# Another slot plan for the work that runs beside the shared FFN in a decoder layer on one core

## The reference

```python
x = x + attn(layernorm(x))            # 32 query heads, 8 key heads, causal, rotary
x = x + xattn(layernorm(x), ctx_2048) # both sides rounded to fp8 and back, then multiplied
x = x + moe(layernorm(x))             # 8 experts, top 1, capacity 256, and a shared FFN
```

```python
q = (xb * (448 / amax)).astype(float8_e4m3fn); xq = q * (amax / 448)   # per 128 numbers
x = x + einsum('emk,enk->emn', xq, wq)                                   # wq from ctx_2048
probs = softmax(xt @ Wg); eidx = argmax(probs)                           # xt = layernorm(x)
pos = cumsum(one_hot(eidx)) ...; keep = pos < 256                        # runs over all tokens
shared = silu(xt @ sw1) * (xt @ sw3) @ sw2                               # 704 hidden columns
```

## Time and profile before

| | us |
|---|---|
| median of 3 runs | 1579.77 (1578.70 to 1581.19) |
| the profiled execution | 1581.1, its span 1579.3 |
| PE busy | 1453.4 (92%) |
| DVE busy | 1205.1 (76%) |
| POOL busy | 1022.9 (65%) |
| ACT busy | 959.4 (61%) |
| granted TensorE clock, mean | 0.97 |

### The profile page before, as it was taken

The page is one execution under the profiler, slowest core; times in us unless marked ns, Lnnn a source line. Parts: engine busy times, 40 slices in busy tenths (PEclk is TensorE's granted clock), DMA queues, the critical chain, the costliest instruction groups (busy, mean ns, idle before and its releaser), DMA issues.

```text
span 1579.3 us, 26942 instructions
## 1 busy us (share of the span) xinstructions
PE 1453.4 (92%) x8617; PEld 1274.5 (81%) x8617; DVE 1205.1 (76%) x2936; ACT 959.4 (61%) x2420; POOL 1022.9 (65%) x1006
## 2 busy tenths in 40 slices
PE   5899999999999999999999997758988887999997
PEld 4788888888878888888888886648888787899996
DVE  7678888887887887887887887976676755577775
ACT  4687777777676787887887886432121213556562
POOL 3787887887777888888898896732121213345555
PEclk9999999999999999999999999888999999899998
DMA  6435534333322433433443432121000003577766
GB/s 205 139 101 165 158 103 128 116 85 109 115 60 59 107 105 90 115 98 95 115 111 86 113 94 67 54 83 60 27 28 28 8 28 124 179 228 223 228 214 237
DMA packets 106812, 177.08 MB, mean 112 GB/s; under 512 B 16886, under 2 KB 38646, under 8 KB 106672
## 3 DMA queue, kind: packets, MB, share of 16 engines
q1 hardware_dynamic: 103920, 166.84, 35.8%
q0 software_dynamic: 2560, 8.25, 1.6%
q10 hardware_dynamic: 192, 0.26, 0.1%
HBM read 97.31 MB, written 31.98 MB: 82 GB/s over the span
## 4 chain that ended last, share of the span: by engine, by line
PE 67%; DVE 15%; ACT 8%; issue 4%; DMA 3%; POOL 2%; SPq 1%; DVEq 0%; ACTq 0%; POOLq 0%
PE bank L429 15%; PE bank L431 14%; PE bank L430 14%; PE bank L481 6%; PE bank L447 4%; PE bank L496 4%; PE bank L497 4%; PE bank L448 4%; ACT P L811 3%; DVE P L1110 2%; PE bank L421 1%; ACT xnx L833 1%; DVE Opair L1145 1%; ACT Otmp L817 1%; DVE work L1059 1%
## 5 line engine op out<-in xcount | busy, mean ns | idle before, releaser
L811 ACT ACTIVATE P<-P,mn 128x512 f32<-128x512 f32 (+3 forms) x512 | 284.8, 557 | 210.5 <-DVE mn L1110 206.6
L1532 POOL TENSOR_TENSOR P<-P,ri 128x128 f32<-128x128 f32 (+3 forms) x512 | 361.4, 737 | 22.4 <-DVE ri L1099 22.3
L1110 DVE CUSTOM_DVE_ANT_0 P<-bank,mask 128x512 f32<-128x512 f32 (+3 forms) x512 | 236.6, 480 | 97.2 <-PE bank L448 95.6
L1151 DVE TENSOR_TENSOR PTl<-bank,PTh 128x512 fp32r<-128x512 f32 (+1 forms) x384 | 229.8, 599 | 33.5 <-ACT PTh L823 30.9
L481 PE MATMUL bank<-ident,P 128*128 128x128 f32 x1280 | 202.6, 273 | 2.5 <-POOL P L1532 2.5
L823 ACT ACTIVATE PTh<-bank 128x512 fp32r<-128x512 f32 (+1 forms) x384 | 197.9, 516 | 6.3 <-PE bank L481 3.2
L447 PE MATMUL bank<-KT,QT 128*128 128x256 f32 (+2 forms) x512 | 188.7, 369 | 10.9 <-DVE mn L1110 10.9
L496 PE MATMUL bank<-PTh,VS 128*128 128x256 f32 (+2 forms) x512 | 163.2, 329 | 13.0 <-DVE PTl L1151 8.9
L429 PE MATMUL bank<-XT,Wh 128*128 128x512 f32 x384 | 162.8, 424 | 9.3 <-DVE XT L1081 3.5
L448 PE MATMUL bank<-KT,QT 128*128 128x256 f32 (+2 forms) x512 | 166.3, 325 | 0.0
L497 PE MATMUL bank<-PTl,VS 128*128 128x256 f32 (+2 forms) x512 | 156.9, 327 | 0.0
(11 more groups left out here) (202 smaller groups left out, 4231.9 us busy)
## 6 DMA issues: line engine op xcount, KB each, us to landing
RW<-in_wf SPq DMA_DIRECT2D x170, 256.0 KB, 3.1
QT<-qh SPq DMA_DIRECT2D x256, 64.0 KB, 2.0
QT<-ql SPq DMA_DIRECT2D x252, 64.0 KB, 2.0
Oraw<-in_wo SPq DMA_DIRECT2D x16, 512.0 KB, 5.3
KT<-KT SPq DMA_DIRECT2D x32, 256.0 KB, 3.0
xnx<-in_ctx SPq DMA_DIRECT2D x32, 256.0 KB, 3.5
Wraw<-in_wqkv SPq DMA_DIRECT2D x9, 768.0 KB, 5.0
saved<-Wh SPq DMA_DIRECT2D x7, 768.0 KB, 3.5
```

The costliest lines, as they stand in the source:

```text
L811: e.activation(pq, pq, ACT.Exp, bias=mn[:, z, qb:qb + 1], scale=-1.0, accum_out=rs[:, z, qb:qb + 1]).then_inc(a_exp, 1)
L1110: e.tensor_tensor_reduce(P[:, z, off[qb]:off[qb] + k], bank[n % 2][:, 0:k], mask[:, 512 - k:512], -0.125, BIG, ALU.add, ALU.min, mn[:, z, ...
L1151: e.tensor_tensor(pt_part(PTl, part), bank[2 + part][:, 0:128 * n].rearrange("p (m n) -> p m n", n=128), pt_part(PTh, part).bitcast(F32), ...
L1532: e.tensor_tensor(pq, pq, ri[:, z, qb:qb + 1].to_broadcast([128, n]), ALU.mult).then_inc(g_norm, 1)
```

## The change

Only numbers in `slots()` change. The instructions are the same ones, and their operands too. For batch 0 nothing moves but its `place`, by one slot. For batches 1 to 3, with s the base slot:

| stage | before | after |
|---|---|---|
| context_turn i | s - 4, - 3, - 2, 0 | s - 9 + i |
| cross_round i | s - 1 + i | s - 7 + 2i |
| cross_turn i | s + 1 + i | s - 5 + 2i |
| cross_product i | s + 2 + i | s - 4 + 2i |
| stats2 i, norm2 | s - 13 + i, s - 7 | s - 12 + i, s - 8 |
| rstd3, norm3, route_turn | s + 6, + 7, + 9 | s + 4, + 5, + 7 |
| logits, choose | s + 12, + 14 | s + 10, + 12 |
| place | s + 19 (b = 3: s + 15) | s + 17 (b = 3: s + 14) |

So for batch 2 (s = 16) the roundings stand in slots 9, 11, 13 and 15, the cross turns in 11, 13, 15 and 17, the products in 12, 14, 16 and 18. The core of the diff:

```diff
-            plan(s - 13 + i if b else s - 3 + i // 2, "stats2", b, i)
-            plan(s + 1 + i, "cross_turn", b, i)
-            plan(s + 2 + i, "cross_product", b, i)
-            plan(s - 1 + i, "cross_round", b, i)
...
+            if b:
+                plan(s - 12 + i, "stats2", b, i)
+                plan(s - 9 + i, "context_turn", b, i)
+                plan(s - 7 + 2 * i, "cross_round", b, i)
+                plan(s - 5 + 2 * i, "cross_turn", b, i)
+                plan(s - 4 + 2 * i, "cross_product", b, i)
...
+        plan(s - (8 if b else 2), "norm2", b)
+        plan(s + (4 if b else 6), "rstd3", b)
+        plan(s + (14 if b == NB - 1 else 17 if b else 18), "place", b)
```

More of the change, by code:

```diff
@@ L43, in slots @@
         for i in range(TB):
-            plan(s - 13 + i if b else s - 3 + i // 2, "stats2", b, i)
-            plan(s + 1 + i, "cross_turn", b, i)
-            plan(s + 2 + i, "cross_product", b, i)
-            plan(s - 1 + i, "cross_round", b, i)
[L48 to L57, removed]
+            if b:
[4 more added lines that the diff above has]
+                plan(s - 4 + 2 * i, "cross_product", b, i)
+            else:
+                plan(s - 3 + i // 2, "stats2", b, i)
+                plan(s - 4 + i + i // 3, "context_turn", b, i)
+                plan(s - 1 + i, "cross_round", b, i)
+                plan(s + 1 + i, "cross_turn", b, i)
+                plan(s + 2 + i, "cross_product", b, i)
+            plan(s + (5 if b else 7) + i // 2, "norm3", b, i)
+            plan(s + (7 if b else 9) + i // 2, "route_turn", b, i)
+        plan(s - (8 if b else 2), "norm2", b)
+        plan(s + (4 if b else 6), "rstd3", b)
+        plan(s + (10 if b else 12), "logits", b)
+        plan(s + (12 if b else 14), "choose", b)
+        plan(s + (14 if b == NB - 1 else 17 if b else 18), "place", b)
     for i in range(2):
```

## The result

| | before | after |
|---|---|---|
| median of 20 runs each | 1580.6 (1578.7 to 1584.6) | 1586.1 (1580.1 to 1591.2) |
| ratio, 95% interval | | 1.0029 (1.0018 to 1.0039) |
| the profiled execution, its span | 1581.1, 1579.3 | 1580.8, 1579.0 |
| granted clock, mean of that execution | 0.97 | 0.971 |
| PE, DVE busy | 1453.4, 1205.1 | 1453.1, 1201.9 |

The forecast was 1574. The last two rows of the table say little; the one of the profiled execution says something new: in the changed kernel it is one of the fastest. Its 20 runs spread over 11 us, and they follow the mean granted clock: the spans average 1578.7 us at 0.973 (2 runs), 1580.8 at 0.971 (4), 1582.3 at 0.970 (2), 1583.9 at 0.969 (2), 1585.1 at 0.968 (8) and 1588.8 at 0.966 (2). Span times mean clock is an estimate of the time at the full clock.

What follows compares the result with a forecast made beforehand. PE, 92% busy, bounds the kernel, so its idle or slow stretches in the FFN count. Removing 39.6 us and adding 33.4 nets -6.2 us: 1573.6 against the median, taken as 1574, range 1561 to 1587.

Steps and rivals of the forecast that it cites:

- What the change removes: PE's waits between 1067 and 1306 us go, -25.1 us, with the low clock behind them, -10.2; moved context turns -1.4.
- all four kinds: PE waits: first cross turn 11.6 us, `place` 3.8, product behind `place` 7.6, first FFN step of a batch 2.1.
- The read-out behind a rounding: In the FFN, eight products wait 2.0 us each for DVE's late read-out, 16 us; 17.5 with batch 1's other waits.
- The third turns: Slots 7, 8, 23, 24: third turn waits 1.75 or 2.95 us for the first's read-out; with clock falls +12.8 us.
- The clock: Behind the eight product waits in the FFN the sum let the granted clock stand, adding nothing.
- Rival One: The eight product waits lower the clock, 1.7 us each: 1587 if all, about 1580 if three or four; chance 0.30.
- Ahead of the FFN: Before x = 0, a rounding and four more read-outs start the FFN 3.1 us later; bounds -1 to +6.
- The prediction's other sum, 1576.5: The whole sum if POOL's port sharing stretched the rounding ahead of the FFN by 2.9 us.
- Where the experts begin: At the experts' first turn, `place` wait of 1.42 us goes and tokens' wait shrinks by 1.5: gain 2.9 us.
- rival Four: The start ahead of the FFN grows by 6 us and the end gives only 1: 1578.5; chance 0.15 with rival three.

Runs made afterwards that it cites:

- the early context turns: Changed kernel with the first three context turns of batches 2 and 3 three slots earlier: 1570.69 us, ratio 0.9934.
- the last kernel: Changed kernel with context turns early, batches 1 and 2 begun later, turns and products one slot later, batch 3's routing and row loads early: 1556.06 us, ratio 0.9848.

## Why the prediction was wrong

**What the change removes** was right in kind, and in size for the waits: all four kinds went, but for 0.44 us. The low clock that went with them was one fall more than the sum had, since in batch 1 it lasted 6.8 us (length, then PE, PEld, DVE, ACT and POOL busy, clock, in the kernel before):

```profile
1091.90:1098.70 6.80, 5.28 (x15) 4.34 (x16) 6.56 (x12) 1.01 (x2) 4.74 (x5) 0.50 0.00 1
```

**The read-out behind a rounding** was right in place and nearly in size: eight waits, 15.7 us in all (16.4 in the two rows less 0.61 at x = 0, and rounding), forecast 8 x 1.85 = 14.8 as the profile shows idle time. What is above is one wait of 2.99 where 1.9 were expected. There POOL's rounding lies beside DVE's subtraction for the FFN, which takes 1.11 us; the same instruction took 0.39 us six microseconds before, with POOL idle:

```profile
1085.59 0.39 DVE L1352 TENSOR_TENSOR Hl<-hm,Hh 128x256 fp32r<-128x256 f32 x1
1091.63 1.11 DVE L1352 TENSOR_TENSOR Hl<-hm,Hh 128x256 fp32r<-128x256 f32 x1
```

```profile
1091.20 1.26 POOL L1580 TENSOR_TENSOR work<-work 128x512 f32<-128x512 f32 x1 [10.68 <-DVE work L1185]
```

The subtraction ends at 1092.74, 0.28 us behind POOL's instruction (1092.46). Of the 1.1 us in question 0.72 is this stretch, and the rest is the subtraction itself, which doesn't stand in the slot of the 1.81 us wait. The Trainium skill, page "SBUF — State Buffer", section "Who interferes with whom", says that a DVE instruction with two SBUF inputs contends with a GpSimd instruction that reads SBUF. The trace agrees, by 0.72 us here. The prediction had named the effect for the start and as a bound here, and had put it into neither number.

**The third turns** were right: 1.50 and 2.75 twice each, forecast 1.75 and 2.95, and a fall behind one of the two longer ones in the profile.

**The clock** is the step that failed most: the sum let it stand after the eight product waits, a term of nothing. The prediction asked of each wait whether it is long enough to bring the clock down, found 2.00 us with no fall and 2.17 us with one, put its eight waits of 1.85 on the safe side, and left the falls to a rival with 0.30. But no safe side shows at such a length. In one execution 1.81 and 1.78 us brought it down and 1.83 and 1.78 did not. The very wait that the prediction took for its safe side, the 2.00 us at 462.12 in the attention, which the change doesn't touch, is followed by the lower clock in the changed kernel's profile (12 matmuls where the kernel before gets 21 through):

```profile
461.37 0.47 PE L434 MATMUL bank<-XT,Wh 128*128 128x512 f32 x1 [2.02 <-DVE XT L1086]
462.30:465.60 3.30, 3.30 (x12) 2.83 (x11) 1.17 (x5) 1.41 (x4) 3.30 (x4) 0.50 0.50 165
```

Over many executions about half of the eight bring it down, by the price of 1.7 us a fall: filling them with work gave 7.8 us back. Two rows on either side of a supposed edge were read as the edge. The right value for such waits was an expected share of falls, four of eight, times 1.7 us: 6.8 us, and the forecast would have been 1580.8. Rival One had this price, near 1580 for three or four.

**Ahead of the FFN** the sum said +3.1, and it was +5.9. PE's rows there, and DVE's between them:

```profile
1064.05 1.09 PE L426 MATMUL bank<-ident,XN 128*128 128x128 f32 x4 [6.25 <-issue]
1070.09 1.09 PE L426 MATMUL bank<-ident,XN 128*128 128x128 f32 x4 [2.40 <-issue]
1072.64 0.55 PE L434 MATMUL bank<-XT,Uh 128*128 128x256 f32 x1 [0.61 <-issue]
```

```profile
1058.81 1.48 DVE L1064 TENSOR_SCALAR work<-X,mv,rstd 128x512 f32<-128x512 f32 x1
1062.92 0.43 DVE L1185 TENSOR_SCALAR work<-work 128x512 f32<-128x512 f32 x1
1066.41 2.97 DVE L1343 TENSOR_TENSOR Dl<-RW,Dh 128x512 fp32r<-128x512 f32 x2
```

```profile
1058.30 1.71 POOL L1617 TENSOR_TENSOR Dl<-RW,Dh 128x512 fp32r<-128x512 f32 x1
1067.12 3.40 POOL L1617 TENSOR_TENSOR Dl<-RW,Dh 128x512 fp32r<-128x512 f32 x2
```

The chain of seven turns was as drawn. Late are two of DVE's steps, both beside POOL's splitting: the rounding, forecast to end at 1061.5, ends at 1063.3 (it begins 0.8 us late, and its first instruction takes 1.48 us; it took 0.54 in the earlier trace rows), and the two pieces take 2.97 where two lone ones of 0.68 would take 1.4. These 1.8 and 1.6 us cover the 2.8 between 1069.8 and 1072.64. The prediction's other sum, 1576.5, stretched the rounding by 2.9 us; its instructions grew by 0.9, and the pieces by 1.6. That batch 1's work is what stands in the way is shown: with it moved behind x = 0, the start is 1063.70, and the same first instruction takes 0.54.

**Where the experts begin** I forecast -1.5 for the tokens' wait, and it was +0.5. SP issued the load at 1331.37, 1.4 us earlier than in the earlier trace rows; the tokens let the turn start 0.8 us earlier, and PE got there 1.3 us earlier, so nothing closed. That the schedule sets this wait, and nothing that the load itself needs, is shown: with the stages one to three slots and the load two slots earlier it is gone.

**In the FFN of the profiled execution** the misses nearly cancel, to +0.7 us. Three falls behind product waits, which the sum had at nothing, are +5.1; one fall instead of two behind third turns is -1.7, and the one fall more of before up to -1.7. The idle time in all went from 26.5 to 25.4 us where 26.9 were forecast, -1.5.

So rival One and rival Four both came true in part. From 1573.6 to 1586.1 it is 12.5 us: 2.8 at the start, 0.7 in the FFN, 2.0 and 0.5 at the end, and 5.3 of clock in the median that the profiled execution doesn't have. The last 1.3 are what the sum took off because the profiled execution of before lay above the median of 3 runs; against the median of 20 it lies 0.5 above.

Still open: how often each single wait brings the clock down, for which one profile of each kernel is too few; and which falls the early context turns save.

## What to carry to other kernels

When stages share an in-order engine, list for each slot what that engine does ahead of the one instruction that the busiest engine waits for; moving one culprit away helps only if nothing else of the same length takes its slot. Where several short waits per stage are near the length that has once been seen to drop TensorE's clock, price each with a chance of a fall, and check the spread of the run times against the mean granted clock before trusting one profile; span times mean clock, averaged over the runs, tells the waits of two kernels apart from their clock. And a filler of useless matmuls is a cheap experiment that separates the clock's share of a wait from the wait itself.

## What the runs showed of the hardware

- Idle times of TensorE of equal length (1.78 and 1.78 us, 1.81 and 1.83 us, in slots of the same kind) are followed by the lower clock once and by the full one the other time. The changed kernel's 20 runs range from a mean clock of 0.973 to 0.966 and by 11 us with it; the last kernel, with fewer long waits, stays at 0.976 to 0.979 and within 3 us in its 5 runs.
- The same wait in the attention, 2.00 us before and 2.02 after, was followed by a clock of 1.00 in one profile and of 0.50 in the other.
- Idle time that is filled with matmuls nobody needs made the kernel 7.8 us faster; its span times mean clock stayed the same (1534.9 and 1534.8 us).
- DVE's instructions took longer beside POOL: 1.11 instead of 0.39 us, 1.48 instead of 0.54, and 2.97 for two pieces of 0.7 each.
